# Row maxima split by GpSimd and turned by VectorE in 32x32 blocks, in place of a TensorE transpose and a ScalarE copy

## The chip, the cores and the metric

The kernel runs on one core of a Trainium2 chip. The metric is the device time of one execution in microseconds (us), the median of several runs. Lower is better.

## The reference

One transformer layer over 1024 tokens of width 512, attention and feed-forward side by side, both added to the input:

```python
xn = layernorm(x)
q, k, v = bitnet(xn, Wq), bitnet(xn, Wk), bitnet(xn, Wv)   # sign weights times a scale per output
scores = q k^T / sqrt(16)            # 32 query heads, 8 key heads, 4 query heads to a key head
attn = softmax(scores) v
out = x + bitnet(attn, Wo) + (silu(xn gate^T) * (xn up^T)) down^T      # hidden width 1792
```

## The kernel before

The kernel is written engine by engine, and each engine works through its own instructions in the order written. Semaphores tie the engines together: an instruction waits until a counter has reached a value.

**Two passes over the scores.** The softmax needs the maximum of every row of scores before the exponentials. So the scores are computed twice. The first pass (`half_rows`, L1144) puts queries on the partitions: one unit is 128 queries of one head against all 1024 keys, in two PSUM banks. VectorE reduces each unit to one column of negated maxima, `nmx` (L842, a 128x1024 reduction). The second pass (`scores`, L1250) puts keys on the partitions, ScalarE takes the exponential (L709), and TensorE multiplies the result by the values (`times_values`, L1319). The maximum enters the second pass as two extra rows of the query operand `qst`: a high and a low fp16 part, against a constant row in the keys. So the column of maxima on 128 partitions has to become a row.

**How a column becomes a row before.** Sixteen units make one block: four heads by 512 queries. When the sixteen columns of a block are done, TensorE transposes `nmx` (128x16) into a PSUM bank (`transpose_max`, L1155), ScalarE scales it into `mxs` (`take_max`, L625), GpSimd writes the high part (L552) and the low part (L554) into `shp`, and the SyncE queue moves the rows into `qst` with four DMAs (`load_shift`, L408). There are 16 such blocks, v = 0 to 15.

**Stages.** First come layer norm, projections and the feed-forward's first half, where three written lists (`pe_order`, `dve_order`, `act_order`) set the order of the steps: `F` is a feed-forward tile, `A` a row-maximum unit, `T` the first transpose. The main loop begins at about 151 us and has 128 steps. A step is one tile of 128 keys for four heads: four score matmuls, four exponentials, the product with the values of the step before, and, up to step 107, two first-pass units for a later block (a *half-step* is one unit with half of the rest). Eight steps are a block. In step 1 of each block (`T_STEP`) TensorE transposes the maxima for the next block. From step 108 (`LATE`) the first pass has only eight units left, one a step (L1293, L969), and TensorE fills its time with the second half of the feed-forward (`down_strips`, L1198). The last transpose stands behind step 115, for the block that begins at step 120. A tail with the output projection ends the kernel.

**Banks.** First-pass units take the bank pairs 0-1 and 2-3 in turn, so TensorE can be at most two units ahead of the reductions (`rows_free`). The four other banks (`RING`) are dealt out to scores, to the value accumulator (`"v"`) and to the transposed maxima (`"t"`), each freed by an earlier use. In step 108 the fourth score tile uses bank 3, and so waits for the last reduction of step 107.

**GpSimd's queue.** GpSimd runs `hidden_low` (L546) for the feed-forward, issues the large load of `wd` (L567), and then has `split_max`, the copy of the next values (L572) and, late, loads for the normalization of the output (`normalize_io`).

Of the kernel before, what the change touches and what calls it, by code (L numbers as in the profile page):

```python
# [27 lines left out]
def layer_kernel(nc, x, wq, wk, wv, wo, wq_rows, wk_rows, wv_rows, wo_rows, sq, sk, sv, so, gate, up, down, sg, su, sd, out,  # L28
# [14 lines left out]
    HI = P // 2  # L43
    UNITS = REP * HALF // P
# [14 lines left out]
                "A17 F20 T0 A18 A19 F21 A20 A21 F22 A22 A23 F23 A24 A25 F24 A26 A27 F25 A28 A29 F26 A30 A31 F27 ")  # L59
# [4 lines left out]
    act_order = ("D0 C0 C1 D1 N1 C2 N2 C3 N0 C4 B5 C5 C6 C7 B4 B2 B0 B1 B3 F0 E0 E1 F1 X0 X1 F2 E3 F3 V2 W0 X3 F4 E4 E5 "  # L64
                 "F5 F6 X4 F7 F8 F9 F10 F11 X5 F12 F13 F14 F15 F16 Y0 F17 Y1 F18 F19 F20 T0 F21 F22 F23 F24 F25 F26 "
# [6 lines left out]
    T_AT = [n for kind, n in pe_order[:pe_order.index(("T", 0))] if kind == "F"][-1]  # L72
# [3 lines left out]
    assert T_AT % 2 == 0 and len(PROJ) == 6  # L76
    assert pe_order.index(("T", 0)) > pe_order.index(("A", UNITS - 1))
# [23 lines left out]
    T_STEP = 1  # L101
# [6 lines left out]
    LATE_T = 0  # L108
# [7 lines left out]
    for step in range(LATE):  # L116
# [21 lines left out]
    assert LATE % TT > T_STEP and ROWS_END - 1 == (2 * NG - 2) * TT + LATE_T_STEP  # L138
    assert LATE + len(QUOTAS) == NG * STEPS and sum(QUOTAS) == len(FILLS) and sum(QUOTAS[:ROWS_END - LATE]) == 2 * FT

    def t_step(block_):

        return LATE_T_STEP if block_ == 2 * NG - 2 else T_STEP

# [20 lines left out]
    with ExitStack() as ctx:  # L165
# [90 lines left out]
        shp = sb("shp", [UNITS, 2, 2, P], F16)  # L256
        mxs = sb("mxs", [UNITS, P], F32)
# [74 lines left out]
        maxT_ready = sem("maxT_ready")  # L332
        max_taken = sem("max_taken")
        shift_step = sem("shift_step")
# [53 lines left out]
        def _(sp):  # L388
# [114 lines left out]
        def _(pool):  # L503
# [30 lines left out]
            nc.gpsimd.memset(vext[:, :, :, :], 1.0).then_inc(consts_ready, 1)  # L534

# [13 lines left out]
            def split_max(v, hf):  # L549

                pool.wait_ge(max_taken, v + 1)
# [4 lines left out]
            for w in range(FU):  # L556
                f, hf = w // 2, w % 2
                if w == T_AT + 1:
                    split_max(0, 0)
# [860 lines left out]
```

## Time and profile before

| what | before |
|---|---|
| median of 3 runs | 501.74 us (500.88 to 502.9) |
| the profiled execution, its own time | 502.01 us |
| its span (first to last recorded instruction) | 500.3 us |
| mean granted TensorE clock | 0.996 of full speed |
| busy: TensorE, VectorE, ScalarE, GpSimd | 96%, 83%, 70%, 19% |

The busy shares are averages over stages with different limits. Durations of two instructions that follow each other can overlap, so the distance from start to start is what an instruction costs its engine; rows that merge several instructions give the stretch from the first start to the last end.

### The profile page before, as it was taken

The numbers are of one execution on the slowest core, as the hardware profiler recorded it, in microseconds if no ns is written. First come the engines' busy times: TensorE is split into PE (matmuls) and PEld (weight loads), VectorE is DVE, ScalarE is ACT, GpSimd is POOL, SyncE is SP. The second block draws the span as 40 slices with busy tenths as digits, with TensorE's granted clock in tenths as the row PEclk, the third lists the DMA queues.
The fourth block names the chain that finished last, engine by engine and source line by source line (L and its number), as shares of the span: only waits on it lengthen the run. The fifth ranks groups of instructions, "written<-read, shape, count | busy, mean of one in ns | idle before, by whom it ended". The sixth has DMA issues, their size and how long they took to land.

```text
span 500.3 us, 10322 instructions
## 1 busy us (share of the span) xinstructions
PE 482.1 (96%) x4186; PEld 163.9 (33%) x4186; DVE 416.9 (83%) x487; ACT 348.3 (70%) x655; POOL 94.6 (19%) x138
## 2 busy tenths in 40 slices
PE   1899999999998999999999999999999999999996
PEld 1564444433332222222222222222222233333442
DVE  7879869676777999999999999999999955224986
ACT  1943643352338999999999999999999978874000
POOL 4212244434323000000000000000000113241021
PEclk9999999999998999999999999999999999999999
DMA  8843673732103702102102211211120124452321
GB/s 269 273 95 98 163 151 42 200 74 25 20 1 54 135 24 64 41 24 64 41 24 65 41 36 50 42 57 29 42 63 24 35 78 112 105 148 80 104 84 43
DMA packets 31302, 39.02 MB, mean 78 GB/s; under 512 B 6608, under 2 KB 20816, under 8 KB 31256
## 3 DMA queue, kind: packets, MB, share of 16 engines
q1 hardware_dynamic: 22232, 27.34, 18.9%
q0 software_dynamic: 8304, 10.95, 11.9%
q8 instruction: 33, 0.54, 0.5%
q10 hardware_dynamic: 720, 0.08, 0.1%
q14 instruction: 13, 0.11, 0.1%
HBM read 33.24 MB, written 10.35 MB: 87 GB/s over the span
## 4 chain that ended last, share of the span: by engine, by line
PE 94%; DVE 3%; ACT 1%; DMA 1%; issue 1%; ACTq 0%; SPq 0%; DVEq 0%
PE ps L1319 28%; PE ps L1135 19%; PE ps L1250 15%; PE ps L1144 10%; PE ps L1211 5%; PE ps L1198 5%; PE ps L1114 4%; PE ps L1353 3%; PE ps L1286 2%; DVE stats L768 1%; ACT room L709 1%; DVE room L790 1%; PE ps L1106 1%; PE ps L1155 1%; DMA hlo<-x 1%
## 5 line engine op out<-in xcount | busy, mean ns | idle before, releaser
L842 DVE TENSOR_REDUCE nmx<-ps 128x1 f32<-128x1024 f32 x248 | 284.1, 1216 | 14.2 <-PE ps L1144 13.9
L709 ACT ACTIVATE room<-ps 128x512 f32<-128x512 f32 x512 | 271.5, 602 | 21.5 <-PE ps L1286 11.0
L1319 PE MATMUL ps<-room,vcur 128*32 128x256 f32 (+1 forms) x1880 | 159.6, 411 | 0.7 <-ACT room L709 0.7
L1144 PE MATMUL ps<-kA,qst 48*128 48x512 f16 x496 | 142.4, 384 | 0.0
L1250 PE MATMUL ps<-qst,kB 50*128 50x512 f16 x432 | 135.6, 385 | 0.6 <-DVE room L941 0.4
L1135 PE MATMUL ps<-room,wf 128*128 128x512 f16 x448 | 100.6, 379 | 0.0
L1319 PEld LDWEIGHTS ps<-room,vcur 128*32 128x32 f32 x1880 | 37.2, 108 | 94.6 <-issue 53.9
L689 ACT ACTIVATE room<-ps,gsc 128x512 f32<-128x512 f32 x28 | 19.3, 688 | 61.8 <-PE ps L1135 61.8
L1135 PEld LDWEIGHTS ps<-room,wf 128*128 128x128 f16 x448 | 42.4, 98 | 55.1 <-issue 7.2
L1250 PEld LDWEIGHTS ps<-qst,kB 50*128 50x128 f16 x432 | 27.7, 93 | 92.6 <-ACT room L709 71.9
L546 POOL TENSOR_TENSOR hlo<-room,hhi 128x512 f16<-128x512 f32 x28 | 34.0, 1216 | 87.2 <-ACT hhi L619 87.2
L552 POOL TENSOR_TENSOR shp<-mxs,ones 16x128 f16<-16x128 f32 x16 | 8.1, 503 | 223.6 <-ACT mxs L625 223.6
L941 DVE SCALAR_TENSOR_TENSOR room<-ps,usc,room 128x512 f32<-128x512 f32 x28 | 20.9, 746 | 13.9 <-issue 10.0
L1144 PEld LDWEIGHTS ps<-kA,qst 48*128 48x128 f16 x496 | 26.1, 94 | 7.7 <-issue 7.5
L1198 PE MATMUL ps<-wd,hhi 128*32 128x512 f16 x224 | 22.3, 379 | 0.0
L1198 PE MATMUL ps<-wd,hlo 128*32 128x512 f16 x224 | 22.3, 379 | 0.0
L1211 PE MATMUL ps<-wd,hhi 128*128 128x512 f16 x56 | 21.2, 379 | 0.0
L1211 PE MATMUL ps<-wd,hlo 128*128 128x512 f16 x56 | 21.2, 379 | 0.0
L619 ACT CAST hhi<-room 128x512 f16<-128x512 f32 x28 | 17.2, 613 | 1.0 <-DVE room L941 1.0
L1114 PE MATMUL ps<-room,sgn 128*128 128x512 f16 x80 | 17.8, 379 | 0.0
L982 DVE TENSOR_TENSOR y<-y,ga 128x1024 f32<-128x1024 f32 (+1 forms) x5 | 5.0, 998 | 15.0 <-DMA ga<-r_scratch 15.0
L512 POOL TENSOR_TENSOR room<-room,parts 128x512 f32<-128x512 f32 x7 | 9.6, 1377 | 39.0 <-DVE room L998 27.1
(136 smaller groups left out, 319.4 us busy)
## 6 DMA issues: line engine op xcount, KB each, us to landing
qst<-q_scratch SPq DMA_DIRECT2D x32, 192.0 KB, 3.6
o_scratch<-osb SPq DMA_DIRECT2D x16, 256.0 KB, 2.3
q_scratch<-parts SPq DMA_DIRECT2D x12, 256.0 KB
hlo<-x SPq DMA_DIRECT2D x8, 256.0 KB, 4.6
parts<-x POOLq DMA_DIRECT2D x8, 256.0 KB, 3.9
wf<-gate POOLq DMA_DIRECT2D x14, 128.0 KB, 3.8
wf<-up POOLq DMA_DIRECT2D x14, 128.0 KB, 5.9
wd<-down POOLq DMA_DIRECT2D x1, 1792.0 KB, 13.5
```

Of the source, the lines that this page charges most:

```text
L546: nc.gpsimd.tensor_tensor(hlo[:, f, hf * HALF:(hf + 1) * HALF], hb[:, w % 2, :], hhi[:, f, hf * HALF:(hf + 1) * HALF], ALU.subtract).then_ ...
L689: nc.scalar.activation(gt[:, n % 2, :], ps[:, 4 + 2 * (n % 2), :], ACT.Silu, scale=gsc[:, f:f + 1]).then_inc(gt_ready, 1)
L709: nc.scalar.activation(probs[:, s % 2, r, :], ps[:, bank_of(gp, s, i), :], ACT.Exp, scale=gam_reg[par][r]).then_inc(scores_free, 1)
L842: nc.vector.tensor_reduce(nmx[:, hf, idx:idx + 1], bank_pair(idx % 2), AX.X, ALU.max, negate=True).then_inc(rows_free, 1)
L941: nc.vector.scalar_tensor_tensor(out=hb[:, n % 2, :], in0=ps[:, 5 + 2 * (n % 2), :], scalar=usc[:, f:f + 1], in1=gt[:, n % 2, :], op0=ALU. ...
L1114: mm = nc.tensor.matmul(ps[:, 2 * (n % 2) + hf, :], sgn[:, c, c0:c0 + P], xs[:, c, hf * HALF:(hf + 1) * HALF], start=(c == 0 and xs is xhi ...
L1135: mm = nc.tensor.matmul(ps[:, 4 + 2 * (w % 2) + z, :], wf[:, f % WF_BUFS, z, c * P:(c + 1) * P], xs[:, c, hf * HALF:(hf + 1) * HALF], star ...
L1144: return nc.tensor.matmul(ps[:, 2 * (idx % 2) + b, :], qst[low:low + KROWS, par, hf, head, qt * P:(qt + 1) * P], kA[low:low + KROWS, par, ...
L1198: mm = nc.tensor.matmul(ps[32 * c:32 * c + 32, FILL_BANKS[i % 2], :], (hhi, hlo)[part][:, f, lo:lo + 32], wd[:, f, :], start=(f == 0 and p ...
L1211: mm = nc.tensor.matmul(ps[:, DOWN_BANKS[i - FILL], :], (hhi, hlo)[part][:, f, i * P:(i + 1) * P], wd[:, f, :], start=(f == 0 and part == ...
L1250: nc.tensor.matmul(ps[:, bank_of(gp, s, i), :], kB[low:low + SROWS, par, kt % (TT // 2) * P:(kt % (TT // 2) + 1) * P], qst[low:low + SROWS ...
L1319: mm = nc.tensor.matmul(ps[32 * r:32 * r + 32, values_bank(step_ // TT), of], vcur[:, par, key_tile(r, j), :], probs[:, s % 2, r, of], sta ...
```

## The change

The transpose leaves TensorE, and the copy leaves ScalarE. GpSimd now reads `nmx` itself (128 partitions x 16) and makes three small results: the scaled maxima in fp32 (`mxs`), their high parts in fp16, and their low parts, the two fp16 halves side by side in `mxp` (128x32). VectorE turns `mxp` in square blocks of 32x32 into `shp` (`turn_max`), which leaves queries 32b to 32b+31 on the partitions of block b: 16 rows of high parts, then 16 of low parts. The rows therefore arrive in `qst` with eight DMAs a block, one for each of four blocks and two copies, each of 32 pieces of 64 bytes. VectorE's new instruction stands between the two reductions of step 1 of each block; the first one stands ahead of `F20` in `dve_order`, the last behind the reduction of step 115. The `"t"` uses leave the ring of banks.

```diff
@@ the lists of steps (of pe_order, dve_order and act_order one line each)
-                "A17 F20 T0 A18 A19 F21 A20 A21 F22 A22 A23 F23 A24 A25 F24 A26 A27 F25 A28 A29 F26 A30 A31 F27 ")
+                "A17 F20 A18 A19 F21 A20 A21 F22 A22 A23 F23 A24 A25 F24 A26 A27 F25 A28 A29 F26 A30 A31 F27 ")
...
-                 "A17 F20 A18 A19 F21 A20 A21 A22 A23 F22 F23 A24 A25 A26 F24 A27 A28 F25 A29 F26 A30 A31 F27 ")
+                 "A17 T0 F20 A18 A19 F21 A20 A21 A22 A23 F22 F23 A24 A25 A26 F24 A27 A28 F25 A29 F26 A30 A31 F27 ")
...
-                 "F5 F6 X4 F7 F8 F9 F10 F11 X5 F12 F13 F14 F15 F16 Y0 F17 Y1 F18 F19 F20 T0 F21 F22 F23 F24 F25 F26 "
+                 "F5 F6 X4 F7 F8 F9 F10 F11 X5 F12 F13 F14 F15 F16 Y0 F17 Y1 F18 F19 F20 F21 F22 F23 F24 F25 F26 "
@@ ring of banks
-        if j == T_STEP:
-            taken.append(("t", block_ + 1))
-        elif j == T_STEP + 1:
-            freed.append(("t", block_ + 1))
@@ tiles
-        shp = sb("shp", [UNITS, 2, 2, P], F16)
-        mxs = sb("mxs", [UNITS, P], F32)
+        unlift = sb("unlift", [P, UNITS], F32)
+        mxs = sb("mxs", [P, UNITS], F32)
+        mxp = sb("mxp", [P, 2 * UNITS], F16)
+        shp = sb("shp", [P, 2, SQ], F16)
@@ load_shift (sync)
-                for low in (0, HI):
-                    for part in range(2):
-                        row = low + KROWS + part
-                        dst = qst[row:row + 1, par, hf].rearrange("p h n -> p (h n)")
-                        sp.dma_start(dst, shp[:, hf, part, :]).then_inc(shift_loaded[par][hf], 16)
+                for row in (KROWS, HI + KROWS):
+                    dst = qst[row:row + 2, par, hf].rearrange("p h (t b n) -> p (h t) b n", b=P // SQ, n=SQ)
+                    for b in range(P // SQ):
+                        sp.dma_start(dst[:, :, b, :], shp[b * SQ:(b + 1) * SQ, hf, :]).then_inc(shift_loaded[par][hf], 16)
@@ split_max (gpsimd)
-                pool.wait_ge(max_taken, v + 1)
-                nc.gpsimd.tensor_tensor(shp[:, hf, 0, :], mxs[:, :], ones[0:UNITS, :], ALU.mult).then_inc(shift_step, 1)
-                pool.wait_ge(shift_step, v + 1)
-                nc.gpsimd.tensor_tensor(shp[:, hf, 1, :], mxs[:, :], shp[:, hf, 0, :], ALU.subtract).then_inc(shift_ready, 1)
+                pool.wait_ge(rows_free, 2 + (v + 1) * UNITS)
+                pool.wait_ge(shift_ready, v)
+                nc.gpsimd.tensor_tensor(mxs[:, :], nmx[:, hf, :], unlift[:, :], ALU.mult).then_inc(split_step, 1)
+                nc.gpsimd.tensor_tensor(mxp[:, 0:UNITS], nmx[:, hf, :], unlift[:, :], ALU.mult).then_inc(split_step, 1)
+                pool.wait_ge(split_step, 2 * (v + 1))
+                nc.gpsimd.tensor_tensor(mxp[:, UNITS:2 * UNITS], mxs[:, :], mxp[:, 0:UNITS],
+                                        ALU.subtract).then_inc(split_ready, 1)
@@ take_max (scalar), transpose_max (tensor): gone, with their calls and waits
@@ vector
+            def turn_max(v, hf):
+                dve.wait_ge(split_ready, v + 1)
+                nc.vector.transpose(shp[:, hf, :], mxp[:, :]).then_inc(shift_ready, 1)
@@ step_rows (vector)
                     row_max(ga_ * (2 * UNITS) + hf * UNITS + 2 * j, hf, 2 * j)
+                    if j == 1:
+                        turn_max(step // TT + 1, 1 - hf)
                     row_max(ga_ * (2 * UNITS) + hf * UNITS + 2 * j + 1, hf, 2 * j + 1)
...
+                    if step == ROWS_END - 1:
+                        turn_max(2 * NG - 1, 1)
```

VectorE's program, from the end of the feed-forward stage into the main loop. A row is a line of the kernel, the operation, what it writes and reads, its shape and how often it repeats; L842 and L826 are the 128x1024 reductions, L941 and L930 the feed-forward product. Before:

```order
L842 TENSOR_REDUCE nmx<-ps 128x1
L941 SCALAR_TENSOR_TENSOR room<-ps,usc,room 128x512
L842 TENSOR_REDUCE nmx<-ps 128x1 x2
L941 SCALAR_TENSOR_TENSOR room<-ps,usc,room 128x512
L842 TENSOR_REDUCE nmx<-ps 128x1 x216
L969 TENSOR_REDUCE nmx<-ps 128x1 x2
```

The same place of the changed kernel:

```order
L826 TENSOR_REDUCE nmx<-ps 128x1
L930 SCALAR_TENSOR_TENSOR room<-ps,usc,room 128x512
L826 TENSOR_REDUCE nmx<-ps 128x1 x2
L930 SCALAR_TENSOR_TENSOR room<-ps,usc,room 128x512
L826 TENSOR_REDUCE nmx<-ps 128x1 x3
L832 STREAM_TRANSPOSE shp<-mxp 128x32
L826 TENSOR_REDUCE nmx<-ps 128x1 x16
L832 STREAM_TRANSPOSE shp<-mxp 128x32
```

The 216 reductions in a row are now cut by a transpose behind the third, and then behind every sixteenth.

GpSimd's program at the same place (L546 and L538 are `hidden_low`, L567 and L562 the load of `wd`). Before:

```order
L565 COPY vcur<-vext 128x256
L546 TENSOR_TENSOR hlo<-room,hhi 128x512
L567 DMA wd<-down 128x14x512
L552 TENSOR_TENSOR shp<-mxs,ones 16x128
L554 TENSOR_TENSOR shp<-mxs,shp 16x128
L572 COPY vcur<-vext 128x256
```

The same place of the changed kernel:

```order
L560 COPY vcur<-vext 128x256
L538 TENSOR_TENSOR hlo<-room,hhi 128x512
L562 DMA wd<-down 128x14x512
L545 TENSOR_TENSOR mxs<-nmx,unlift 128x16
L546 TENSOR_TENSOR mxp<-nmx,unlift 128x16
L548 TENSOR_TENSOR mxp<-mxs,mxp 128x16
L567 COPY vcur<-vext 128x256
```

The split still stands behind the last `hidden_low` and the issue of `wd`, but VectorE's second transpose now waits for it, where only the DMA queue waited before.

## Rows read from the trace of the kernel before

**Rows 1.** The page: busy time of the engines, and the chain that ended last

```profile
PE 482.1 (96%) x4186; PEld 163.9 (33%) x4186; DVE 416.9 (83%) x487; ACT 348.3 (70%) x655; POOL 94.6 (19%) x138
PE 94%; DVE 3%; ACT 1%; DMA 1%; issue 1%; ACTq 0%; SPq 0%; DVEq 0%
```

**Rows 2.** Windows: busy us (and instructions) from 158.6 to 399.5 us

```profile
158.60:399.50 240.90, 240.83 (x2553) 61.84 (x2553) 240.41 (x212) 230.83 (x450) 15.30 (x36) 1.00 0.21 48
```

**Rows 3.** Line L842 in that window: duration ns min/median/max, then its idle time

```profile
L842 DVE TENSOR_REDUCE nmx<-ps x212: 1214/1215/1226, 158.7 to 399.0; 128x1 f32<-128x1024 f32 x106
...
  PE ps L1144: 1.3, 2
```

**Rows 4.** Timeline of VectorE (start us, us): inside a block, and across a transpose

```profile
196.23 15.92 DVE L842 TENSOR_REDUCE nmx<-ps 128x1 f32<-128x1024 f32 x14
...
192.72 3.59 DVE L842 TENSOR_REDUCE nmx<-ps 128x1 f32<-128x1024 f32 x3
```

**Rows 5.** Timeline of TensorE around the transpose of one block

```profile
191.16 0.64 PE L1319 MATMUL ps<-room,vcur 128*32 128x256 f32 x8
...
192.27 0.64 PE L1319 MATMUL ps<-room,vcur 128*32 128x256 f32 x8
...
193.48 0.64 PE L1319 MATMUL ps<-room,vcur 128*32 128x256 f32 x8
...
194.05 0.28 PE L1155 MATMUL ps<-ident,nmx 128*16 128x128 f32 x1
...
194.96 0.64 PE L1319 MATMUL ps<-room,vcur 128*32 128x256 f32 x8
```

**Rows 6.** Timeline of VectorE: small operations back to back

```profile
24.04 0.17 DVE L878 TENSOR_TENSOR cqk<-mag,scqk 128x5 f32<-128x5 f32 x1
24.12 0.28 DVE L879 TENSOR_SCALAR vdiag<-ident,mag 128x128 f32<-128x128 f32 x1
...
38.60 0.19 DVE L904 TENSOR_SCALAR gam<-ps 128x32 f32<-128x32 f32 x1
38.70 0.18 DVE L905 TENSOR_TENSOR own_gam<-ps,own 128x32 f32<-128x32 f32 x1
```

**Rows 7.** Timeline of GpSimd: small operations, the second waiting for the first

```profile
3.17 0.18 POOL L529 TENSOR_SCALAR_AFFINE_SELECT own<-own 128x8 f32<-128x8 f32 x1
3.43 0.19 POOL L532 TENSOR_SCALAR_AFFINE_SELECT own<-own 128x8 f32<-128x8 f32 x1
3.56 1.80 POOL L534 MEMSET vext<- 128x2048 f32 x1
```

**Rows 8.** The chain that ended last, at the first transpose (start us, us)

```profile
122.51 0.11 PE ps L1155
```

**Rows 9.** Timeline of VectorE and GpSimd where the main loop begins

```profile
152.06 3.48 DVE L842 TENSOR_REDUCE nmx<-ps 128x1 f32<-128x1024 f32 x3
158.67 19.43 DVE L842 TENSOR_REDUCE nmx<-ps 128x1 f32<-128x1024 f32 x17 [1.10 <-PE ps L1144]
156.16 1.15 POOL L567 DMA_DIRECT2D wd<-down  x1
```

**Rows 10.** Timeline from step 108 on: weight loads of TensorE, and GpSimd

```profile
400.27 0.09 PEld L1286 LDWEIGHTS ps<-qst,kB 50*128 50x128 f16 x1 [0.35 <-DVE nmx L842]
...
420.17 0.09 PEld L1155 LDWEIGHTS ps<-ident,nmx 128*16 128x16 f32 x1 [0.44 <-DVE nmx L969]
420.38 0.11 PEld L1286 LDWEIGHTS ps<-qst,kB 50*128 50x128 f16 x4
...
421.47 1.35 POOL L552 TENSOR_TENSOR shp<-mxs,ones 16x128 f16<-16x128 f32 x1 [0.32 <-ACT mxs L625]
...
432.56 0.11 PEld L1286 LDWEIGHTS ps<-qst,kB 50*128 50x128 f16 x4 [0.42 <-issue]
```

**Rows 11.** Line L408, the DMAs of the last rows, 420 to 430 us

```profile
L408 SPq DMA_DIRECT2D qst<-shp x4: 509/590/597, 423.3 to 425.2; - x4
...
DMA to landing us min/median/max: 3.0/3.3/6.7
```

More of the change, by code:

```diff
@@ L43, in layer_kernel @@
     HI = P // 2
+    SQ = 32
     UNITS = REP * HALF // P
@@ L71, in layer_kernel @@
     pe_order, dve_order, act_order = steps_of(pe_order), steps_of(dve_order), steps_of(act_order)
-    T_AT = [n for kind, n in pe_order[:pe_order.index(("T", 0))] if kind == "F"][-1]
+    SPLIT_AT = [n for kind, n in dve_order[dve_order.index(("A", UNITS - 1)):] if kind == "F"][0]
     NORM_GROUPS = [(0, 4), (4, 8)]
@@ L75, in layer_kernel @@
     SUM_AT = [n for kind, n in pe_order[pe_order.index(("S", 1)):] if kind == "A"][0]
-    assert T_AT % 2 == 0 and len(PROJ) == 6
-    assert pe_order.index(("T", 0)) > pe_order.index(("A", UNITS - 1))
+    assert len(PROJ) == 6 and dve_order.index(("T", 0)) > dve_order.index(("F", SPLIT_AT))
     assert [n for kind, n in pe_order if kind in "FU"] == list(range(FU))
@@ L137, in layer_kernel @@
     QUOTAS = [4] * 4 + [3] * 4 + [7] * 12
-    assert LATE % TT > T_STEP and ROWS_END - 1 == (2 * NG - 2) * TT + LATE_T_STEP
+    assert ROWS_END - 1 == (2 * NG - 2) * TT + LATE_T_STEP
     assert LATE + len(QUOTAS) == NG * STEPS and sum(QUOTAS) == len(FILLS) and sum(QUOTAS[:ROWS_END - LATE]) == 2 * FT
-    def t_step(block_):
-        return LATE_T_STEP if block_ == 2 * NG - 2 else T_STEP
     def fills_of(step):
@@ L534, in _ @@
             nc.gpsimd.memset(vext[:, :, :, :], 1.0).then_inc(consts_ready, 1)
+            nc.gpsimd.memset(unlift[:, :], 1.0 / LIFT).then_inc(pool_step, 1)
+            pool.wait_ge(pool_step, 5)
             pool.wait_ge(x_loaded[TT - 1], 16)
@@ L619, in hidden_high @@
                 nc.scalar.copy(hhi[:, f, hf * HALF:(hf + 1) * HALF], hb[:, n % 2, :]).then_inc(hhi_ready, 1)
-            def take_max(v, bank):
-                act.wait_ge(maxT_ready, v + 1)
-                act.wait_ge(shift_ready, v)
-                nc.scalar.activation(mxs[:, :], ps[0:UNITS, bank, 0:P], ACT.Copy, scale=1.0 / LIFT).then_inc(max_taken, 1)
             splits = 0
@@ L702, in exps @@
                 step = gp * (2 * STEPS) + s
-                if j == t_step(step // TT) + 1 and not (last and s >= STEPS + TT):
-                    block_ = gp * 4 + s // TT
-                    take_max(block_ + 1, LATE_T if step >= LATE else ring_bank["t", block_ + 1])
                 act.wait_ge(probs_free, step + 1)
@@ L956, in _ @@
                     row_max(n, n // UNITS, n % UNITS)
+                elif kind == "T":
+                    turn_max(0, 0)
             def step_rows(gp, s, last):
@@ L1151, in rows @@
                 half_rows(par, hf, idx, 1).then_inc(rows_ready, 1)
-            def transpose_max(v, hf, bank):
-                pe.wait_ge(rows_free, 2 + (v + 1) * UNITS)
-                nc.tensor.transpose(ps[0:UNITS, bank, 0:P], nmx[:, hf, :], ident[:, :]).then_inc(maxT_ready, 1)
             for kind, n in pe_order:
@@ L1300, in late_scores @@
                     down_strips(*fill)
-                if step == ROWS_END - 1:
-                    transpose_max(2 * NG - 1, 1, LATE_T)
             def times_values(gp, s, part, cut):
```

29 lines of the change are left out of this document (7 added, 22 removed).

## The prediction

> **What bounds the kernel now.** I read the page first. By busy time TensorE leads with 96%, and 94% of the chain that ended last is TensorE's [rows 1]. Read alone, that says that a transpose taken off TensorE is a gain. But a busy TensorE can be one that is being paced, so I looked next at the stretch in which 13 of the 16 transposes lie, from 158.6 to 399.5 us. There VectorE is busy 240.41 of 240.90 us, as full as TensorE, and ScalarE 230.83 [rows 2]. The reader is to see that three engines are nearly full at once, and that the question is which has no slack at all.
>
> The list of VectorE's reductions answers it. Its 212 reductions of this stretch have two waits, 1.3 us together, of which 1.10 us stand before the first [rows 3, 9]. Inside a block 14 reductions take 15.92 us; the last of them lasts 1.215, so they start every (15.92 - 1.215) / 13 = 1.131 us [rows 3, 4]. TensorE's half-step, which makes one unit for VectorE, starts every 1.11 us (191.16 to 192.27) [rows 5]. So inside a block VectorE is the slower, by 0.02 us a unit, and TensorE gains 16 x 0.02 = 0.34 us on it. TensorE then loses time: 1.21 us for the half-step from 192.27 to 193.48, and 1.48 us for the one with the transpose, from 193.48 to 194.96 [rows 5]. That is 0.10 + 0.37 = 0.47 us a block, a little more than the 0.34 that it gained. The difference shows on VectorE as a small gap: three reductions across a transpose take 3.59 us, where 2 x 1.131 + 1.215 = 3.48 would do, so 0.11 us are lost once a block [rows 4]. In sum: from 158.67 (its first start) to 399.0 (its last) are 240.3 us, and 211 steps of 1.131 are 238.7, so all gaps together are 1.6 us [rows 3, 9].
>
> VectorE's end is also what counts: at step 108 TensorE's fourth score tile waits 0.35 us for the last of these reductions [rows 10]. Whatever VectorE gains or loses before 399 us is handed on whole. Ahead of the main loop, and after step 108, TensorE sets the pace.
>
> **The change, part by part.** Times are us, added to the profiled execution's 502.01 (span 500.3), which lies 0.27 above the median of 501.74; the difference is then applied to the median.
>
> *Transpose and copy gone inside the stretch.* TensorE gets 0.37 us a block back. It can use only what VectorE lets it: VectorE needs 16 x 1.131 = 18.10 us for a block, TensorE then 16 x 1.11 + 0.10 = 17.86. TensorE's remaining loss (0.10) is smaller than its gain (0.34), so it stays ahead, and VectorE's gaps close: -1.6. ScalarE's copy lay beside this and gives nothing of its own.
>
> *A transpose on VectorE, 14 times in the full stretch (v = 1 to 14).* Nothing hides it. The trace has no such operation. The nearest rows are small operations back to back: one on 5 elements starts 0.08 before the next, one that reads 32 elements 0.10 before the next, though they last 0.17 and 0.19 [rows 6]. A 32x32 block cannot be written before it has been read whole, so I add 32 elements once more; by the 5- and 128-element rows one costs (0.28 - 0.17) / 123 = 0.9 ns, together 0.03. I take 0.13. The lower bound is 0.08; the upper one, with no overlap at either side, is 0.19 + two times 0.03 = 0.25. A gain is excluded: the engine has to issue it. For 13 of them (v = 2 to 14): 13 x 0.13 = +1.7. The one for v = 1 comes next.
>
> The same row bears on a rule of the Trainium skill, "VectorE: DVE Perf Modes", section "The DRAIN you can't avoid": the next VectorE operation does not start until the pipeline of the one before is empty. The trace does not agree for these sizes, as the 0.17 us operation is followed after 0.08. By the rule a turn would cost its duration (0.19 and 0.03 by the rows above) and the sum be higher by 14 x (0.22 - 0.13) = 1.3 us; by the row it stays as given. The same page's section "The three transpose paths" has 311 ns for a 128x128 bf16 transpose on VectorE; less 96 columns at 0.9 ns that makes an estimate of 0.22 us for the duration of one of 32 columns, which no run shown here tests.
>
> *A new wait at the main loop's start.* VectorE's second transpose stands behind the third reduction of the row that begins at 152.06, which ends at 155.54 [rows 9]. It waits for GpSimd's split of v = 1, which stands behind the issue of the `wd` load; that issue ends at 156.16 + 1.15 = 157.31 [rows 9]. GpSimd's three small operations cost 0.13 for the first (3.43 to 3.56), 0.26 for the second, whose result the third waits for (3.17 to 3.43), and 0.19 for the third [rows 7]: done at 157.89, seen by VectorE at about 157.95. The turn leaves the engine free at 158.08. Behind it in VectorE's queue are the fourth reduction, which now starts at 158.08, and the fifth, which started at 158.67 [rows 9] and now starts at 158.08 + 1.13 = 159.21, so +0.54. TensorE stalls behind it for its bank pair, which costs nothing more, as VectorE has the pace from here on. The bound above: GpSimd's first operation beside DMA issues once lasted 1.35 instead of 0.45 [rows 10]. That long, it would add 1.35 - 0.19 = 1.2.
>
> In the other blocks the split has three reductions (3.4 us) for its 0.6 us, so no wait is seen.
>
> *First transpose (ahead of `F21` on TensorE):* -0.11, its piece on the chain [rows 8]. VectorE's turn ahead of `F20` falls into idle time.
>
> *Last transpose (behind step 115):* TensorE's weights for it load at 420.17 and those of the next scores at 420.38 [rows 10]: -0.21. VectorE now waits about 2 us here for GpSimd, with the low part of the first output tile and the first output of the feed-forward queued behind; neither is awaited within that time, as the bank that the latter frees is next written in step 120.
>
> *Eight DMAs for four.* An issue is 0.59 [rows 11], so the queue is held 2.4 us longer a block. A block lasts 18 us, and the rows are due in the next one: hidden, except perhaps for the last block (below).
>
> **Sum:** -1.6 + 1.7 + 0.5 - 0.1 - 0.2 = +0.3. Predicted: 501.74 + 0.3 = **502.0 us**.
>
> **The rivals.** *(a) TensorE is the bound, as the page's chain has it.* Then each of 13 blocks gives 0.37, and the two other transposes 0.32: -5.1, 496.6 us. For it speaks the chain [rows 1]; against it, that VectorE has only 1.6 us of gaps to give in the whole stretch [rows 3]. Chance 5%.
>
> *(b) The turn is dear, and the kernel slower.* Place: VectorE, after the third reduction of each block. Each 0.1 us above 0.13 costs 1.4 us. It decides from +2.5 us on, that is from 0.13 + 2.2 / 14 = 0.29 us a turn, above my upper bound: it would need that a transpose also holds back the reduction behind it. At 0.35 the time is 505.1. For it: no transpose is in the trace. Against it: every small operation there is followed after half its duration [rows 6]. Chance 9%.
>
> *(c) The rows come late for the last block.* If the split begins at 421.47 as before and takes 0.6, the turn is done near 422.3, the eighth DMA is issued at 422.3 + 7 x 0.59 = 426.4, and lands 3.3 us later by the median, 6.7 by the slowest [rows 11]: 429.7 to 433.1. Step 120 needs it at 432.56 [rows 10]. With the 1.35 us operation it is 434.3, so 1.7 late: 503.7 us. Chance 5%.
>
> The forecast's own case (gaps closed, turn 0.08 to 0.25) has the remaining 81%.
>
> **How the numbers follow.** A measurement of this kernel tells about 0.5% (2.5 us) from no change. Turn at 0.08: 0.3 - 14 x 0.05 = -0.4, 501.3 us. Turn at 0.25: +2.0, 503.7. The three runs of before spread by about 1 us around their median, so I let the range reach 0.5 beyond: 500.8 to 504.2. (c) lies inside it, (a) and (b) outside: about 15%. Faster by over 0.5%: only (a), 5%. Slower by over 0.5%: (b), 9%, and with it both of the upper bounds at once, which I put into the same 9%. Within 0.5%: 86%.
>
> **What would show it.** Right: in the main loop each block has 16 reductions at 1.131 us and one turn, with 0.08 to 0.25 us more from the third reduction's start to the fourth's than 1.131, no gap elsewhere; block lengths of 18.18 to 18.35 us; one wait of about 2.4 us on VectorE for GpSimd near 155 to 158, one near 420. Wrong: blocks of 17.9 us or less (then (a)); blocks of 18.4 or more (then (b), or gaps that did not close); TensorE waiting at step 120 for a DMA (then (c)). If the block is 18.3 and gaps are still there, my reading that TensorE stays ahead is the step that failed.

## The result, and the profile after

| what | before | after |
|---|---|---|
| median | 502.65 us (500.88 to 503.81, 11 runs) | 504.61 us (502.72 to 507.57, 11 runs) |
| ratio, with its 95% interval | | 1.0046 [1.0029, 1.0063] |
| the profiled execution, its own time | 502.01 us | 502.72 us |
| its span, mean granted TensorE clock | 500.3 us, 0.996 | 500.7 us, 1.000 |

The change costs 0.46%, about 2.0 us. I had forecast +0.3, that is 502.0 us, with a range up to 504.2, so the result lies just above the range. Of the 2.6 us between 502.0 and 504.61, 0.9 is not the change: I had added it to the median of three runs of before, 501.74, and the median of eleven is 502.65. The two profiled executions are only 0.71 us apart. The study is about the rest: where do 2 us come from, when one pair of traces shows 0.7?

The page of after, its line of busy time and its chain; they answer to [rows 1]:

```profile
PE 480.7 (96%) x4170; PEld 166.3 (33%) x4170; DVE 417.0 (83%) x503; ACT 347.8 (69%) x639; POOL 89.9 (18%) x155
DVE 51%; PE 46%; POOL 1%; issue 1%; DMA 1%; ACT 0%; SPq 0%; ACTq 0%; DVEq 0%; POOLq 0%
```

Busy times hardly move, but the chain does: VectorE has 51% of it now, where it had 3%. The reader is to see that the loop was VectorE's before as well [rows 2]; that the chain followed TensorE only because the small gaps of VectorE led it there is my reading of it, which no run tests by itself.

The window of the main loop, which answers to [rows 2], then the reductions in it and the turn (L832) over the whole span, which answer to [rows 3]:

```profile
158.45:399.45 241.00, 239.76 (x2531) 64.02 (x2531) 241.00 (x227) 229.98 (x435) 11.84 (x48) 1.00 0.22 50
```

```profile
L826 DVE TENSOR_REDUCE nmx<-ps x213: 1171/1206/1214, 158.4 to 399.4; 128x1 f32<-128x1024 f32 x107
...
L832 DVE STREAM_TRANSPOSE shp<-mxp x16: 190/193/211, 120.9 to 423.0; 128x32 f16<-128x32 f16 x16
```

VectorE is busy for all 241.00 us. The gaps of before are gone. The timeline of VectorE across one block, which answers to [rows 4]:

```profile
194.71 0.19 DVE L832 STREAM_TRANSPOSE shp<-mxp 128x32 f16<-128x32 f16 x1
194.83 18.14 DVE L826 TENSOR_REDUCE nmx<-ps 128x1 f32<-128x1024 f32 x16
212.90 0.19 DVE L832 STREAM_TRANSPOSE shp<-mxp 128x32 f16<-128x32 f16 x1
```

From turn to turn are 212.90 - 194.71 = 18.19 us; before it was 18.21. A turn lasts 0.19 and is followed after 0.12 (0.125). So the reduction behind a turn starts 1.256 behind the one ahead of it, 0.125 more than 1.131. The next one follows after 1.099, 0.03 less, which leaves 0.09 for a turn, net. So the loop went as forecast. The place where it begins did not. The timelines of VectorE and of GpSimd there answer to [rows 9]:

```profile
148.23 2.35 DVE L826 TENSOR_REDUCE nmx<-ps 128x1 f32<-128x1024 f32 x2
...
152.33 3.48 DVE L826 TENSOR_REDUCE nmx<-ps 128x1 f32<-128x1024 f32 x3
158.31 0.21 DVE L832 STREAM_TRANSPOSE shp<-mxp 128x32 f16<-128x32 f16 x1 [2.51 <-POOL mxp L548]
158.45 3.44 DVE L826 TENSOR_REDUCE nmx<-ps 128x1 f32<-128x1024 f32 x3
```

```profile
156.43 1.12 POOL L562 DMA_DIRECT2D wd<-down  x1
157.58 0.23 POOL L545 TENSOR_TENSOR mxs<-nmx,unlift 128x16 f32<-128x16 f32 x1
157.75 0.23 POOL L546 TENSOR_TENSOR mxp<-nmx,unlift 128x16 f16<-128x16 f32 x1
158.06 0.22 POOL L548 TENSOR_TENSOR mxp<-mxs,mxp 128x16 f16<-128x16 f32 x1
```

The split stands behind the issue of `wd`, and VectorE waits 2.51 us for it. This is the wait that I forecast, at nearly the time that I forecast (158.31 for 157.95, and this execution reached the row of three 0.27 later). What I had wrong is what it is compared with. The windows of this place, of before and then of after (columns: window; its length; busy time and instructions of TensorE, its weight loads, VectorE, ScalarE, GpSimd; granted clock; DMA share; GB/s):

```profile
153.00:155.00 2.00, 1.26 (x12) 0.47 (x12) 2.00 (x3) 2.00 (x6) 0.00 (x0) 1.00 0.00 0
155.00:157.00 2.00, 2.00 (x19) 0.43 (x12) 1.19 (x2) 2.00 (x4) 1.94 (x2) 0.51 0.00 0
157.00:159.00 2.00, 2.00 (x17) 0.38 (x13) 0.90 (x2) 1.00 (x4) 1.21 (x4) 0.63 0.37 42
```

```profile
153.00:155.00 2.00, 1.06 (x10) 0.42 (x12) 2.00 (x3) 2.00 (x5) 0.00 (x0) 1.00 0.00 0
155.00:157.00 2.00, 2.00 (x24) 0.59 (x22) 0.80 (x1) 2.00 (x5) 1.67 (x2) 1.00 0.00 0
157.00:159.00 2.00, 1.22 (x13) 0.25 (x9) 0.69 (x2) 1.86 (x4) 1.51 (x5) 1.00 0.29 25
```

In the profiled execution of before, TensorE was granted half its clock (1.2 of 2.4 GHz) from 155.1 to 158.5, just here. In that of after it was granted the full clock. Most of the 1.10 us idle before the fifth reduction [rows 9] was the price of that stretch and not a property of the kernel (e3 below has 0.40 there at full clock). I had taken it as given and let the new wait hide in it.

### The profile page after: what moved, and what is told of

Read it like the earlier page. It is cut to its first block, busy times and chain, and to the rows that moved or that the text cites. A ratio compares the mean times of both kernels' runs of the same rounds, so it can differ in the third digit from the quotient of the medians.

```text
span 500.7 us, 10356 instructions
## 1 busy us (share of the span) xinstructions
PE 480.7 (96%) x4170; PEld 166.3 (33%) x4170; DVE 417.0 (83%) x503; ACT 347.8 (69%) x639; POOL 89.9 (18%) x155
## 4 chain that ended last, share of the span: by engine, by line
DVE 51%; PE 46%; POOL 1%; issue 1%; DMA 1%; ACT 0%; SPq 0%; ACTq 0%; DVEq 0%; POOLq 0%
DVE nmx L826 48%; PE ps L1128 19%; PE ps L1197 5%; PE ps L1184 5%; PE ps L1298 4%; PE ps L1109 4%; PE ps L1332 3%; PE ps L1267 2%; PE ps L1137 2%; DVE stats L752 1%; PE ps L1047 1%; PE ps L1101 1%; DMA hlo<-x 1%; POOL hlo L538 0%; DVE room L774 0%
## 5 line engine op out<-in xcount | busy, mean ns | idle before, releaser
L826 DVE TENSOR_REDUCE nmx<-ps 128x1 f32<-128x1024 f32 x248 | 283.3, 1206 | 11.8 <-PE ps L1137 11.8
L1137 PE MATMUL ps<-kA,qst 48*128 48x512 f16 x496 | 134.7, 382 | 1.5 <-DVE nmx L826 1.5
L1234 PEld LDWEIGHTS ps<-qst,kB 50*128 50x128 f16 x432 | 31.2, 94 | 92.2 <-ACT room L693 79.3
L538 POOL TENSOR_TENSOR hlo<-room,hhi 128x512 f16<-128x512 f32 x28 | 34.0, 1216 | 87.6 <-ACT hhi L614 87.6
L545 POOL TENSOR_TENSOR mxs<-nmx,unlift 128x16 f32<-128x16 f32 x16 | 3.6, 222 | 219.0 <-DVE nmx L826 218.9
L930 DVE SCALAR_TENSOR_TENSOR room<-ps,usc,room 128x512 f32<-128x512 f32 x28 | 20.8, 744 | 13.7 <-issue 11.8
L1137 PEld LDWEIGHTS ps<-kA,qst 48*128 48x128 f16 x496 | 24.3, 93 | 9.5 <-issue 7.6
L962 DVE TENSOR_REDUCE nmx<-ps 128x1 f32<-128x1024 f32 x8 | 9.8, 1222 | 8.2 <-PE ps L1274 8.2
```

Of the source, the lines that this page charges most:

```text
L538: nc.gpsimd.tensor_tensor(hlo[:, f, hf * HALF:(hf + 1) * HALF], hb[:, w % 2, :], hhi[:, f, hf * HALF:(hf + 1) * HALF], ALU.subtract).then_ ...
L826: nc.vector.tensor_reduce(nmx[:, hf, idx:idx + 1], bank_pair(idx % 2), AX.X, ALU.max, negate=True).then_inc(rows_free, 1)
L930: nc.vector.scalar_tensor_tensor(out=hb[:, n % 2, :], in0=ps[:, 5 + 2 * (n % 2), :], scalar=usc[:, f:f + 1], in1=gt[:, n % 2, :], op0=ALU. ...
L1137: return nc.tensor.matmul(ps[:, 2 * (idx % 2) + b, :], qst[low:low + KROWS, par, hf, head, qt * P:(qt + 1) * P], kA[low:low + KROWS, par, ...
L1234: nc.tensor.matmul(ps[:, bank_of(gp, s, i), :], kB[low:low + SROWS, par, kt % (TT // 2) * P:(kt % (TT // 2) + 1) * P], qst[low:low + SROWS ...
```

## The experiments

The kernels ran in three sets (the first with e1 and e3, the second with e4, e5, e6 and e8, the third with e7, e9 and e8 again). A set shares one chip and its runs of the kernel before (medians 502.46, 502.50, 502.71); ratios are to those. Beside the times I read one piece of each trace: from the start of the last first-pass reduction ahead of the main loop (`A31`) to the start of the fifth reduction of the loop. That piece holds the wait and the place of the first turn of the loop. In before its first row is the second of these two, which starts 1.13 behind 147.96, at 149.09; the fifth reduction starts at 158.67 [rows 9], so the piece is 9.57:

```profile
147.96 2.35 DVE L842 TENSOR_REDUCE nmx<-ps 128x1 f32<-128x1024 f32 x2
```

In after the piece is 10.18 (149.36 to 159.54).

| kernel | median, us | ratio [95%] | that piece, us | half clock in it |
|---|---|---|---|---|
| before, again | 503.17 | 1.0015 [0.9997, 1.0034] | 9.57 | yes |
| before + idle turn (e3) | 502.94 | 1.0008 [0.9992, 1.0025] | 8.37 | no |
| before + wait (e6) | 503.73 | 1.0015 [0.9990, 1.0039] | 9.89 | no |
| before + GpSimd padding (e7) | 503.45 | 1.0004 [0.9982, 1.0026] | 9.57 | yes |
| before, 16 DMAs a block (e4) | 512.12 | 1.0171 [1.0120, 1.0222] | 9.58 | yes |
| after, again | 505.34 | 1.0050 [1.0026, 1.0075] | 10.19 | no |
| after, first turn at step 4 (e1) | 503.12 | 1.0028 [1.0010, 1.0046] | 8.02 | no |
| after, first turn at step 2 (e5) | 502.50 | 0.9998 [0.9973, 1.0022] | 8.02 | no |
| after, split ahead of the load (e8) | 503.27, 503.79 | 1.0011 [0.9981, 1.0041], 1.0029 [1.0008, 1.0050] | 8.01, 8.01 | no |
| e8 + wait put back (e9) | 504.55 | 1.0030 [1.0008, 1.0052] | 9.90 | yes |

**Both kernels again.** No edit.

> The kernel before once more, to see the TensorE clock and the time of each of its runs. In the profiled executions the changed kernel's span is only 0.4 us longer (500.7 against 500.3), but over the timed runs it is 2 us longer. Theory A (TensorE's clock): half-clock stretches cost the changed kernel more than the kernel before; then runs of the kernel before at a mean clock of 0.995 to 0.996 stay near 502 to 502.7 and those of the changed kernel near 504.5. Theory B (the chip): the profiled execution of the changed kernel was simply a fast one, and the kernel before also has runs about 2 us faster when its clock never falls; then this kernel at a mean clock of 1.0 comes near 500.5 to 501 and at 0.996 near 502.5.

> The changed kernel once more, for its runs and for a second trace. Theory A: at a mean clock of 1.0 near 502.7 to 504, at 0.995 to 0.996 near 504.5, and the trace shows a half-clock stretch lying on the chain. Theory B: the same times by clock, but the kernel before shows the same distance between its clocks. Ratio to the kernel before expected by both: 1.003 to 1.006.

The difference is there again (1.0050 against 1.0015). Neither theory is met in its numbers: the runs of before at 0.995 to 0.996 took 503.0 to 503.9 us, where A had 502 to 502.7, and those at 0.998 to 0.999 took 501.6 to 503.4, where B had 500.5 to 501 at full clock. The trace of after shows something that its first one didn't, on VectorE's timeline:

```profile
158.47 3.44 DVE L826 TENSOR_REDUCE nmx<-ps 128x1 f32<-128x1024 f32 x3
162.63 1.23 DVE L826 TENSOR_REDUCE nmx<-ps 128x1 f32<-128x1024 f32 x1 [0.72 <-PE ps L1137]
164.08 6.90 DVE L826 TENSOR_REDUCE nmx<-ps 128x1 f32<-128x1024 f32 x6 [0.23 <-PE ps L1137]
```

and in its windows:

```profile
157.00:159.00 2.00, 1.24 (x13) 0.25 (x9) 0.67 (x2) 1.87 (x4) 1.53 (x5) 1.00 0.27 24
159.00:161.00 2.00, 1.30 (x11) 0.31 (x11) 2.00 (x3) 0.39 (x1) 0.00 (x0) 0.73 1.09 145
161.00:163.00 2.00, 2.00 (x20) 0.33 (x12) 1.28 (x2) 0.98 (x3) 0.00 (x0) 0.50 1.14 174
```

Now the half-clock stretch lies behind the wait (159.9 to 163.3), inside the loop, and costs 1.15 us of its own: the loop from the fifth reduction to the last of step 107 takes 241.03 us for 239.88 in the first trace.

**e1, the first turn later.** After, with the turn for v = 1 three steps later:

```diff
-                    if j == 1:
+                    if j == (1 if step > TT else 4):
```

> The changed kernel with VectorE's second turn (v = 1) three steps later, behind the ninth instead of the third reduction of the main loop's row, so that it no longer waits for GpSimd. Nothing is left out. The wait of 2.7 us near 155 to 158 us goes, and the reductions behind it start about 0.9 us earlier in the changed kernel's trace, so the span falls by 0.5 to 1.0 us. Theory A says more: the stall at the main loop's start is where the clock falls with a price, so the median falls by 1.5 to 2 us, back to the kernel before. Rival: only the wait itself goes, 0.5 to 1.0 us, and the rest of the loss stays.

The piece shrinks from 10.18 to 8.02 us, and the time is lower than that of after in the same set, by 2.2 us by the medians and by 502.46 x 0.0022 = 1.1 by the ratios. But the rows come late now: the last of the eight DMAs is issued at 169.17 (163.81 in after), their semaphore is complete at 172.18, TensorE's first weight load of the next block starts at 172.24 after 1.27 us without one (0.41 is usual), and VectorE has a gap behind it.

```profile
172.24 0.09 PEld L1234 LDWEIGHTS ps<-qst,kB 50*128 50x128 f16 x1 [1.27 <-issue]
```

The span is 500.6 us, only 0.1 below that of after, where I had expected 0.5 to 1.0: the piece gives 2.2 back, but the late rows cost 0.7 of it in the loop (240.54 us for 239.88), and this execution began its first reduction 1.35 us later (68.95 for 67.60).

**e3, the turn alone, in before.** An idle turn in step 1 of every block of the kernel before:

```diff
+                    if j == 1:
+                        nc.vector.transpose(spare[:, :], mxp[:, :])
```

> The kernel before, with nothing removed, and on VectorE one more 32x32-block transpose of a constant tile in step 1 of each block, between the two reductions, where the changed kernel has its own. It waits for nothing and nobody waits for it. If the turn is paid out of the gap that TensorE's transpose leaves on VectorE (0.117 us a block), the gap shrinks to about 0.02 us, the block stays at 18.21 us and the time within 0.1 us of the kernel before. Rival (the turn is paid in addition): block 18.31, time +1.3 us.

Blocks stay at 18.21 us, and the time at 1.0008: the turn fits into VectorE's gap behind TensorE's transpose, and in after blocks are 18.19 with it. The turn is not the cost. And this trace has no half-clock stretch, so it gives what was missing, the start of before's loop at full clock (timeline of VectorE; its own turn delays nothing here, as VectorE then waits 0.18 us for TensorE):

```profile
149.12 2.35 DVE L845 TENSOR_REDUCE nmx<-ps 128x1 f32<-128x1024 f32 x2
...
153.21 3.48 DVE L845 TENSOR_REDUCE nmx<-ps 128x1 f32<-128x1024 f32 x3
156.61 0.20 DVE L969 STREAM_TRANSPOSE spare<-mxp 128x32 f16<-128x32 f16 x1
156.99 1.23 DVE L845 TENSOR_REDUCE nmx<-ps 128x1 f32<-128x1024 f32 x1 [0.18 <-PE ps L1149]
158.61 17.06 DVE L845 TENSOR_REDUCE nmx<-ps 128x1 f32<-128x1024 f32 x15 [0.40 <-PE ps L1149]
```

The fifth reduction begins 5.40 us after the row of three (158.61 - 153.21), where it was 6.61 in before (158.67 - 152.06) [rows 9]. The half-clock stretch was worth 1.2 us of it.

**e4, more and smaller DMAs, in before.** Sixteen row DMAs a block, of 64-byte pieces like those of after:

```diff
-                        dst = qst[row:row + 1, par, hf].rearrange("p h n -> p (h n)")
-                        sp.dma_start(dst, shp[:, hf, part, :]).then_inc(shift_loaded[par][hf], 16)
+                        dst = qst[row:row + 1, par, hf].rearrange("p h (t b n) -> p (h t) b n", b=4, n=32)
+                        for b in range(4):
+                            sp.dma_start(dst[:, :, b, :],
+                                         shp[:, hf, part, b * 32:(b + 1) * 32]).then_inc(shift_loaded[par][hf], 16)
```

> The kernel before with its row moves cut to pieces of 64 bytes: 16 DMAs a block instead of 4, with the 256 pieces that the changed kernel has. Theory (the wait is the cause): no change in the loop, block 18.21 us, within 0.5 us in the median; perhaps 0.2 to 0.5 us more outside the engines' work, since the changed kernel spends 2.0 us outside its span against 1.7 and 0.24 us more behind its last instruction of work, and more DMA instructions are one candidate for that. Rival (small pieces disturb the other transfers): blocks longer than 18.3, +1 us or more.

It costs 1.7%, where I had expected a median within 0.5 us. The rival has its time, but not its mechanism: seven of the thirteen blocks still take 18.21 us, and the others are longer by up to 0.5. The rows are late where the queue has no room. The trace's group of these DMAs, beside the load of `wd`:

```profile
L409 SPq DMA_DIRECT2D qst<-shp x16: 503/589/1088, 160.0 to 169.7; - x16
...
DMA to landing us min/median/max: 2.6/4.6/5.2
```

The last is issued at 169.7, a landing takes up to 5.2 us here, and TensorE waits for these DMAs until 172.46. In the last block it waits for them from 433.26 to 437.25 and stands idle for 2.5 us of that. A half-clock stretch follows, from 438.7 to 442.2 (windows as above):

```profile
436.00:438.00 2.00, 0.69 (x8) 0.30 (x12) 1.00 (x2) 0.21 (x1) 1.38 (x3) 1.00 0.13 18
...
440.00:442.00 2.00, 2.00 (x22) 0.69 (x16) 0.00 (x0) 0.33 (x1) 0.00 (x0) 0.50 0.91 203
```

TensorE sets the pace there, so it costs half its length, 1.7 us. That is the rest of the 4.2 us by which the way from the last reduction of step 107 to the start of the last VectorE operation is longer than in before (102.00 for 97.76). The loop is 1.5 longer. This execution took 508.33; what the median's further 4 us are, no trace shows. Eight issues, as in after, take half as long, and after shows neither.

**e5, the first turn one step later.** As e1, at step 2:

```diff
-                    if j == 1:
+                    if j == (1 if step > TT else 2):
```

> The changed kernel with VectorE's turn of v = 1 one step later, behind the fifth reduction of the loop's row. The run with it three steps later showed VectorE waiting 0.55 us near 171 us, where the first late block begins; the theory is that the rows then came late (eight issues of 0.6 us behind the turn). One step later they should be in time: no gap near 171, and the time as with the early split within 0.4 us. Rival: the gap near 171 stays, so it is something else.

This removes the wait for GpSimd. The rows still come a little late, where I had expected them in time: their semaphore is complete at 171.93 (0.97 us on TensorE's weight loads, a gap of 0.17 on VectorE), though the last of them was issued at 164.69, and the loop takes 0.4 us longer than in after. In after itself the last is issued at 163.81 and the semaphore complete at 170.20, 6.4 us later and only 1.25 ahead of the load that needs it; in before, with four DMAs, it is 160.80 and 166.16. The load of `wd`, in flight all this time, lands at 169.94 in after, 171.78 in e5 and 171.81 in e1, each time within 0.4 us of the rows, and in e8, where the rows are issued by 161.29 and complete at 170.56, at 171.19. So the eight small DMAs stay out until about the end of `wd`, and the four of before don't; why is not tested. I had also expected the time of the early split, within 0.4 us; e5's median is 0.8 lower than the first one of e8. The ratio is 0.9998. By moving one instruction of 0.2 us by one step, the changed kernel comes level with the kernel before. The timeline of VectorE:

```profile
153.68 3.48 DVE L826 TENSOR_REDUCE nmx<-ps 128x1 f32<-128x1024 f32 x3
157.50 2.50 DVE L826 TENSOR_REDUCE nmx<-ps 128x1 f32<-128x1024 f32 x2 [0.30 <-PE ps L1137]
159.92 0.20 DVE L832 STREAM_TRANSPOSE shp<-mxp 128x32 f16<-128x32 f16 x1
160.04 12.49 DVE L826 TENSOR_REDUCE nmx<-ps 128x1 f32<-128x1024 f32 x11
172.71 3.49 DVE L826 TENSOR_REDUCE nmx<-ps 128x1 f32<-128x1024 f32 x3 [0.17 <-PE ps L1137]
```

**e6, the wait alone, in before.** Two spare 128x16 products on GpSimd behind the issue of `wd`, and VectorE turns a spare tile in step 1 of the first block, waiting for them:

```diff
+                    if step == 1:
+                        dve.wait_ge(spare_ready, 1)
+                        nc.vector.transpose(spare_out[:, :], spare_mid[:, :])
```

> The kernel before with nothing removed, and only the wait added: GpSimd makes two spare 128x16 products behind the issue of the large load, and VectorE turns the spare tile once, in step 1 of the loop, waiting for them. If that wait is the loss, the kernel before gains it: +1.0 to +2.0 us in the median, with VectorE's stretch at the loop's start at about 10.2 us where no half-clock stretch falls into it, and more runs at a mean clock of 0.996 or less than the third that the kernel before has. Rival (the loss is elsewhere): within 0.5 us of the kernel before.

```profile
152.58 3.48 DVE L853 TENSOR_REDUCE nmx<-ps 128x1 f32<-128x1024 f32 x3
158.27 0.21 DVE L978 STREAM_TRANSPOSE spare_out<-spare_mid 128x32 f16<-128x32 f16 x1 [2.21 <-POOL spare_mid L577]
158.41 7.97 DVE L853 TENSOR_REDUCE nmx<-ps 128x1 f32<-128x1024 f32 x7
```

The piece is 9.89 us for 8.37 in e3, so the wait alone costs 1.5 in the kernel before (its turn follows the third reduction's start by 3.43 us; in after, with three products, by 3.72). The median is 1.2 us above that of the set's runs of before, but the ratio's interval includes 1, so the set's times alone would not settle it; against all 105 runs of before in the three sets (93 beside the variants and the 12 of before again) its mean is 1.0 us higher, with a 95% interval of 0.7 to either side. Runs at a mean clock of 0.996 or less are 4 of 12, a third; I had expected more than that.

**e8, the split ahead of the load.** After, with GpSimd's `split_max(1, 1)` behind the copy of `vcur`, ahead of the last `hidden_low` and of the issue of `wd`:

```diff
                     nc.gpsimd.tensor_copy(vcur[:, 0, :, :], vext[:, :, 0, :]).then_inc(vcur_ready, 1)
+                    split_max(1, 1)
                 hidden_low(w)
...
-                    split_max(gp * 4 + par * 2 + 1, 1)
+                    if gp + par > 0:
+                        split_max(gp * 4 + par * 2 + 1, 1)
```

> The changed kernel with one edit in GpSimd's order: the split of v = 1 stands ahead of the last low part of the hidden layer and of the issue of the large load, where its maxima are complete and GpSimd idles. VectorE's order stays, nothing is left out. Theory (the wait at the main loop's start, with a price that I read too low because the trace of before held a half-clock stretch there): the 3.7 us between the third and the fourth reduction of the loop's row go down to 1.5 or less, the stretch from the last reduction of the feed-forward stage to the fifth of the loop falls from 10.2 us to about 8.0, and the median lies 1.8 to 3 us below the changed kernel, 0 to 0.7 us from the kernel before. Rival (DMA pieces or something else spread over the loop): at most 0.5 us below the changed kernel.

> The changed kernel with the early split once more, beside the one with the wait put back. At a mean clock of 0.998 or more near 501.3, against 502.1 of the kernel before; at 0.996 or less near 503 to 505. Over all runs within 0.5 us of the kernel before.

```profile
153.00 3.48 DVE L828 TENSOR_REDUCE nmx<-ps 128x1 f32<-128x1024 f32 x3
156.40 0.20 DVE L834 STREAM_TRANSPOSE shp<-mxp 128x32 f16<-128x32 f16 x1
```

The wait is gone from VectorE's timeline, the piece is 8.01 us and the span 499.3, the shortest of all. The times follow only in part: against after's 1.0046 and 1.0050 the ratios are 1.0011 and 1.0029. The medians lie 0.8 and 1.1 us above the sets' runs of before, and 1.3 us below after's 504.61 in the first set, where I had expected 1.8 to 3. The second set's six runs at 0.998 or more took 501.9 to 503.9, not 501.3.

**e9, the wait put back.** e8 with the spare products and the waiting turn of e6:

```diff
+            nc.gpsimd.tensor_tensor(spare_mid[:, 0:UNITS], spare_in[:, :], spare_in[:, :], ALU.mult)
+            nc.gpsimd.tensor_tensor(spare_mid[:, UNITS:2 * UNITS], spare_in[:, :], spare_in[:, :],
+                                    ALU.mult).then_inc(spare_ready, 1)
```

> The changed kernel with the early split, and the wait put back by itself: GpSimd makes two spare 128x16 products behind the issue of the large load, and VectorE turns a spare tile once, behind the third reduction of the loop's row, waiting for them. Nothing is left out. If that wait is the changed kernel's loss, this is the changed kernel again: +1.5 to +2.5 us against the early split, and most runs at a mean clock of 0.996 or less (19 of the changed kernel's 23 were, 6 of 12 with the early split). Rival (the number of such runs has another cause): +1.5 us at equal clocks, but no more of the low clocks than before.

The piece is 9.90 us again and the ratio 1.0030. This trace's half-clock stretch begins near 156 and lies in the wait, and the piece is as long as in e6, which has none: there it costs nothing. Against e8 in the same set the medians are 504.55 and 503.79, 0.8 us in the expected direction, where I had expected 1.5 to 2.5. The ratios are 1.0030 and 1.0029, and the difference of the means, 0.7, has a 95% interval of 1.2 to either side: the trace shows the wait, the times of this pair don't. Nor did the low clocks come as expected: 0.996 or less in 5 of 12 runs, against 6 of 12 of e8 beside it.

**e7, a longer GpSimd program, in before.** Thirty-four one-column operations near GpSimd's start:

```diff
+            for i in range(34):
+                nc.gpsimd.memset(spare[:, i:i + 1], 1.0)
```

This asks for the 0.25 us at the kernel's end that after has more.

> The kernel before with 34 more GpSimd instructions (one-column memsets of a spare tile) at the start, where GpSimd waits for the input. It tests where the changed kernel's 0.24 us behind its last instruction of work and 0.27 us outside its span come from. If from the length of GpSimd's program (197 instructions against 163), this kernel has them too: 2.0 us outside the span instead of 1.74, and the end of the span 3.7 instead of 3.5 us behind the last VectorE instruction. Rival (the semaphores, or another engine's program): it has neither.

The stretch from the start of the last VectorE operation to the end of the span is 3.83 us, 3.51 in before and 3.76 in after; the part of the run outside the span is 1.81, 1.73 and 2.00. So a longer GpSimd program gave such an addition inside the span, and at most little outside. But e9, whose GpSimd program is longer than after's, has 3.45 at that place. The cause stays open.

## Why the prediction was wrong, point by point

All sizes are us. The third column is measured at full clock on both sides: after's first trace, against before's profiled execution, except at the loop's start, where e3 stands in for it.

| term | predicted | measured |
|---|---|---|
| first transpose off TensorE | -0.11 | -0.11 (`A0` to `A31`: 81.88 to 81.76) |
| gaps close and 13 turns, in the loop | -1.6 + 1.7 | -0.46 (240.34 to 239.88) |
| wait at the main loop's start | +0.54 | +1.81 (8.37 to 10.18) |
| last transpose off TensorE | -0.21 | -0.24 (last reduction of step 107 to ScalarE's copy of a late output tile: 35.97 to 35.73) |
| the end of the span, and outside it | none | +0.25 and +0.27 |
| sum | +0.3 | +1.5 |

The profiled pair differs by 0.71 only, because before's execution carries 1.2 for its half-clock stretch (9.57 to 8.37) and after's began its first reduction 0.38 later (67.60 for 67.22): 1.5 - 1.2 + 0.4.

**The step that failed is the term "A new wait at the main loop's start", +0.54.** Its mechanism was right: who waits, for whom, until when. Its size was the difference to a start time of 158.67 [rows 9] that came from an execution with half a clock at that place. Against that execution it even came out: by my times the piece would be 10.11 (149.09 to 159.21), and after has 10.18. The warning was in the rows: a mean clock of 0.996, 1.10 us idle before just that reduction, and, in the same view from which the line of [rows 2] is, this line for the stretch ahead of the loop's window, at half the clock:

```profile
156.10:158.20 2.10, 2.10 (x15) 0.43 (x13) 1.22 (x1) 1.17 (x3) 1.38 (x3) 0.50 0.06 5
```

I used only the line of the loop, which begins behind it and shows 1.00. At full clock the term is 1.81, the net of two things: without the wait the piece falls from 8.37 to 8.01 (e8; TensorE's transpose of this block is gone too, for which I had put nothing here), and the wait adds 2.17. e6 puts the wait into before, and the piece grows by 1.5; e9 puts it back into e8, and it grows by 1.9; e1, e5 and e8 take it out of after, and it shrinks by 2.2. So the traces show it in both directions. The times show it where it is taken out of after (the means of e1, e5 and e8 lie 1.5, 2.1 and 1.3 below that of after's 23 runs, each by more than its interval of 0.9 to 1.0, though e5's and e8's ran on other chips than the twelve of after again; and e5 is level with before) and where it is put into before (e6, +1.0), but not in e9 against e8.

**The rest, up to 2.0, goes with the granted clock.** Of the runs of before in the three sets, 42 of 105 have a mean granted clock of 0.997 or less, and they are 1.45 us slower than the other 63 (503.73 to 502.28, means). Of after it is 20 of 23 (505.21, against 503.47 in three). So the difference of the means (504.98 - 502.86 = 2.1) is 1.2 to 1.5 at like clock and 0.47 x 1.45 = 0.7 from the share of such runs. That after has such runs more often is measured; that the wait is what draws them is not. For it: without the wait it is 4 of 12 in e1, 4 of 12 in e5, 13 of 24 in e8, and with it put back 8 of 12 in e9. Against it: e6, before with the wait, has 4 of 12, and by the limit of 0.996 that I had named before the run e9 has only 5 of 12 and e8 12 of 24. So the cause stays open. Why e8 gave less in time (its mean is 1.3 below after's) than in its trace (2 us) is open too; part is that its runs with a low clock lose 2.3 us, more than those of before.

**What a single trace can't price.** Two places differ from execution to execution, and together by as much as the change is worth: the first reduction starts between 67.2 and 69.0 us, and the way from the last reduction of step 107 to the last VectorE operation is 0.5 to 0.9 us longer in e3, e7, e9 and the second e8 than in before, after and the first e8, with TensorE idle for 0.3 to 0.8 us between 450 and 460. That is why I compare pieces and not spans.

**VectorE's pace and the gaps: right.** TensorE stays ahead, all gaps close, and blocks are 18.19 us, inside 18.18 to 18.35. The reading that decided the case, that TensorE's 94% of the chain is paced and not a bound, held; rival (a) would have shown blocks of 17.9.

**The turn: inside its bounds, a little cheaper.** 0.125 us from its start to the next, for 0.13 taken, and 0.09 net, since the reduction after next comes 0.03 sooner. That is the loop's term: 13 x 0.09 = 1.2 for 1.7, less the gaps. Rival (b) is out; e3 shows it once more. The Trainium skill, "VectorE: DVE Perf Modes", section "The DRAIN you can't avoid", would have the turn cost its whole duration. The trace does not agree with that rule taken alone: it lasts 0.19 to 0.21 us and is followed after 0.12. The section itself adds that a next operation that is not held starts earlier, which I had left out; the trace agrees with that. The estimate from the same page's section "The three transpose paths", 0.22 us for the duration, lies close above the measured 0.19 to 0.21.

**Eight DMAs for four: hidden, as forecast.** Rival (c) did not come. The last turn stands at 423.02 and not near 422.3, as GpSimd had a DMA issue of the normalization ahead of the split until 422.27, but the last issue begins at 427.8 and TensorE's load at step 120 has only the usual 0.42 in front. From the reduction of step 107 to the end nothing but the 0.24 changes before the last VectorE operation. e4 shows that the cover ends between 8 and 16 issues, and e1 and e5 that beside the load of `wd` a start one or three steps later is already late. The forecast counted the issues alone; in that block after has 1.25 us left. The wait of VectorE near 420 costs nothing, as forecast.

**The end of the kernel: not in the sum.** 0.5 us that no term had, of which e7 can account for about 0.3.

**The range.** It held the turn's bounds and half a microsecond for the runs. I had written the upper bound of the wait's own price (1.2 more) and then left it to the 9% with rival (b); with it in the range the result would have been inside. But that would have been luck: the bound was for a slow GpSimd operation, and the three took 0.22 to 0.23 us each. It would have been luck as well had the eleven runs' 502.65 been the base: the range would then have reached 505.1 and held 504.61, with the wait still taken for 0.54.

## What to carry to other kernels

Before an idle time of the profile is used as cover for a new wait, read the granted clock of that very stretch: an idle time behind a half-clock stretch belongs to the execution, not to the kernel, and the next run may not have it. A small operation that waits for another engine is priced by what stands ahead of it in *that* engine's queue; here 0.7 us of GpSimd's work behind a 1.1 us DMA issue cost a full engine 1.8 us, and one step's delay of the waiting instruction gave it back. When a profiled pair and the medians disagree, compare the clocks of the runs first, and the pair piece by piece. A forecast of a median wants more than three runs for its base.

## What the runs showed of the hardware

Half-clock stretches of 3.4 us come in some executions of a kernel and not in others, at slightly different places: from 155.1 in before, 156.0 in before again, 159.9 in after again, none there in after or e3. In these three TensorE had been partly idle just ahead (1.24 to 1.37 of 2 us busy), but after (1.22 and 1.31) and e3 (1.38 and 1.33) had the same and kept the full clock. One costs 1.1 to 1.2 us where VectorE has the pace, since TensorE then falls behind, half its length (1.7) where TensorE has the pace (e4), and nothing where it lies in a wait (e9).

A 128x32 fp16 turn in 32x32 blocks lasts 190 to 211 ns, and VectorE's next reduction begins 0.12 us after it. The row DMAs take 0.59 to 0.61 us of their queue each, and those of e4 land after 1.7 us by the median of all, but after 2.6 to 5.2 beside the load of `wd`. Beside the same load the eight DMAs of after were complete 6.4 us behind their last issue, and those of e5 7.2.
